# A three-layer graph network: the first layer's table as pairs of 16-bit parts, and eight node tiles of the next projection made during the first aggregation

## What is computed

```python
def reference(x, src, dst, edge_type_3, W0, b0, W1, q1, k1, b1, W2, q2, k2, b2):
    h = relu(layernorm(x))
    x = x + gcn(h)            # h @ W0, rows gathered by src, times dinv[src]*dinv[dst],
                              # summed by dst (with a loop per node), + b0
    h = relu(layernorm(x))
    h = elu(rgat_conv(h, W1, q1, k1, b1, heads=4))
    x = x + rgat_conv(h, W2, q2, k2, b2, heads=1)
    return x

def rgat_conv(x, W, q, k, b, heads):
    xr = einsum('nd,rdf->rnf', x, W)                   # 3 relations
    oi, oj = xr[etype, dst], xr[etype, src]
    alpha = leaky_relu(oi @ q + oj @ k, 0.2)
    e = exp(alpha - segment_max(alpha, dst)[dst])
    a = e / (segment_sum(e, dst)[dst] + 1e-16)
    return segment_sum(a * oj, dst) + b
```

## Time and profile before

| | us |
|---|---|
| median of 3 runs | 1609.46 |
| lowest, highest | 1606.19, 1611.54 |
| the profiled execution, its span | 1607.11, 1605.3 |
| first gather of the first aggregation | 199.7 |
| keys of layer 1 stored | 460.0 |
| first gather of the second aggregation | 780.1 |
| PE busy, share | 1453.7, 91% |
| GpSimd busy | 1000.9, 62% |
| DVE busy | 901.0, 56% |
| ACT busy | 274.0, 17% |

### The profile page before, as it was taken

How to read it: one execution, slowest core, us unless ns; L and a number is a source line. 1 busy time by engine, 2 the same in 40 slices (tenths; PEclk the granted TensorE clock), 3 DMA queues, 4 the chain that set the end, 5 groups by cost and what they waited for, 6 DMA issues and landing times.

```text
span 1605.3 us, 24837 instructions
## 1 busy us (share of the span) xinstructions
PE 1453.7 (91%) x6446; PEld 878.0 (55%) x6450; DVE 901.0 (56%) x2002; ACT 274.0 (17%) x709; POOL 1000.9 (62%) x1112
## 2 busy tenths in 40 slices
PE   4988999999978999999699999769996999899996
PEld 2545555555566555666455555455553655455553
DVE  8677722334455888888688878406324445223333
ACT  2545300000011333323000124410110011000000
POOL 1599277666537777882477777336656662777673
PEclk9988999999987999899799999858997999899998
DMA  8300498899831131111588888701231111889898
GB/s 319 118 20 21 125 315 305 291 316 312 270 102 23 51 110 47 40 37 41 169 303 278 285 262 257 241 3 32 59 111 31 40 43 50 286 298 308 281 303 269
DMA packets 86811, 271.80 MB, mean 169 GB/s; under 512 B 32156, under 2 KB 32531, under 8 KB 86743
## 3 DMA queue, kind: packets, MB, share of 16 engines
q0 software_dynamic: 51072, 199.44, 39.3%
q1 hardware_dynamic: 34807, 65.62, 11.4%
q10 hardware_dynamic: 864, 5.90, 1.0%
HBM read 239.28 MB, written 31.62 MB: 169 GB/s over the span
## 4 chain that ended last, share of the span: by engine, by line
PE 61%; DMA 14%; POOL 10%; issue 7%; DVE 5%; ACT 1%; DVEq 1%; SPq 0%; POOLq 0%; ACTq 0%; PEldq 0%
PE ps L1293 12%; PE ps L1320 12%; PE ps L1359 12%; DMA ring<-keys,idxr 8%; POOL ring L519 8%; PE ps L1361 6%; PE ps L1362 6%; PE ps L1190 5%; DMA ring<-rows,idxr 3%; PE ps L1111 1%; PE ps L1236 1%; PE ps L1153 1%; PE ps L1254 1%; DVE zw L1020 1%; DVE hn L1017 1%
## 5 line engine op out<-in xcount | busy, mean ns | idle before, releaser
L1320 PE MATMUL ps<-wreg,hT 128*128 128x384 f32 x1440 | 486.7, 501 | 7.3 <-PEq L1313 6.6
L519 POOL DMA_INDIRECT ring<-keys,idxr x312 | 319.2, 1023 | 189.1 <-DMA ring<-keys,idxr 73.6
L488 POOL DMA_INDIRECT ring<-rows,idxr x304 | 303.7, 999 | 168.8 <-PEq L1348 60.9
L1320 PEld LDWEIGHTS ps<-wreg,hT 128*128 128x128 f32 x1440 | 280.6, 196 | 202.2 <-issue 23.5
L1359 PE MATMUL ps<-ring,zw 128*128 x664 | 224.0, 495 | 15.6 <-DVE zw L1088 15.0
L1293 PE MATMUL ps<-ring,zw 128*128 x664 | 221.3, 495 | 9.6 <-DVE zw L909 9.6
L488 POOL DMA_INDIRECT ring<-rows,idx x152 | 144.7, 952 | 97.1 <-PE ps L1293 66.0
L1359 PEld LDWEIGHTS ps<-ring,zw 128*128 128x128 f32 x664 | 124.7, 191 | 108.7 <-issue 34.2
L1086 DVE TENSOR_TENSOR ring<-ring,al x166 | 159.2, 959 | 39.4 <-SPq L406 30.7
L1293 PEld LDWEIGHTS ps<-ring,zw 128*128 128x128 f32 x664 | 127.5, 193 | 98.1 <-issue 15.3
L1091 DVE TENSOR_SCALAR zw<-iota_f,tl,al 128x128 f32<-128x128 f32 x166 | 60.8, 368 | 154.7 <-PE ps L1362 129.7
(11 more groups left out here) (189 smaller groups left out, 1314.0 us busy)
## 6 DMA issues: line engine op xcount, KB each, us to landing
wreg<-in_L_gnn_W SPq DMA_DIRECT2D x11, 2304.0 KB, 9.8
rows<-stage SPq DMA_DIRECT2D x30, 386.0 KB, 2.8
rows<-stage SPq DMA_DIRECT2D x30, 384.5 KB, 2.9
stT<-targets_row ACTq DMA_DIRECT2D x6, 960.0 KB
ring<-keys,idxr POOLq DMA_INDIRECT x312, 2.5
ring<-rows,idxr POOLq DMA_INDIRECT x304, 4.5
rows<-stT SPq DMA_DIRECT2D x10, 384.0 KB, 2.9
xs<-in_x SPq DMA_DIRECT2D x3, 1152.0 KB, 13.4
```

The costliest lines, as they stand in the source:

```text
L488: nc.gpsimd.indirect_dma_start(ring[:, t % (2 * RING), 0:WIDTH[l]], None, rows[l], bass.IndirectOffsetOnAxis(idx[:, t:t + 1], 0)).then_inc ...
L519: nc.gpsimd.indirect_dma_start(kb[:, n % KSEMS, t % KB, 0:4], None, keys[l], bass.IndirectOffsetOnAxis(idxr[:, t:t + 1], 0)).then_inc(k_in ...
L1320: last = mm(ps[:, 2 * (nt % 2) + h, 0:HALF], hT[:, k, nt * P:(nt + 1) * P], wreg[:, r % 2, k, h * HALF:(h + 1) * HALF], start=(k == 0), st ...
```

## The change

1. **The first table in two 16-bit parts.** Per node and tile DVE takes the largest and smallest value of a row (`peaks`), makes a power of two from it (`units`), ACT writes the upper part as f16 (`upper_parts`), DVE the rest as a second f16 (`lower_parts`), and the row stored is upper and lower parts, 768 words as before, with the power of two in the 769th. The parts lie in `hT`, whose layout becomes node tile first. The first table is stored in three lots (`SPLITS`: node tiles 0 to 6, 7 and 8, 9). In the aggregation a slot tile is two one-hots in bf16 from a ring of four pairs, and four 16-bit products in place of two f32 ones; `dinv` of the source is in the parts already. DVE's one-hots no longer wait for `w_used`. A node's own row is added by PE (`open_own`), with a diagonal of the powers from DVE (`begin0`), in place of L886; the bias is added per node tile.
2. **Folds and weight products moved.** PE's folds of relation 0 stand behind the slot tiles of node tiles 0, 1 and 2 (`last_folds`); the wait for the parts stands ahead of node tile 0. `prepare(R - 1)` and the fill of `stage` move from the stage behind the aggregation to DVE's place behind node tile 0; `prepare(1)` now stands behind the lower parts, and the last weight load of layer 2 behind that.
3. **Early products.** In `early`, PE makes relation 0's products for node tiles 0 to 7 (`EARLY` = 8), each behind the turning of the next node tile; DVE makes `rstd` of a node tile with four Newton steps (`inverse_root`); ACT copies out and stores the row (`early_rows`). The stage behind starts with node tile 8. For layer 1 `MAX_AT` and `MASKS_AT` are set anew.

The core of the diff:

```diff
+          1: {17: (0,), 19: (1,), 21: (2,), 23: (3,), 24: (4,), 26: (5,), 27: (6,), 28: (7,), 29: (8, 9, 10, 11)}}
-MASKS_AT = [(SURE_PAIRS - 3) * (h + 1) // LAST_PAIRS_AT + 2 for h in range(LAST_PAIRS_AT)]
+EARLY = 8
+MASKS_AT = [(SURE_PAIRS - 3) * max(h + 1 - 2 * EARLY, 0) // (LAST_PAIRS_AT - 2 * EARLY) + 2 for h in range(LAST_PAIRS_AT)]
+SPLITS = ((0, 1, 2, 3, 4, 5, 6), (7, 8), (9,))
...
-        tbank = [2 * (n % 2) for n in range(NF)] + [0] * NT + [2 * (n % 2) for n in range(KT)] + [4] * NT + [4 + 2 * (n % 2) for n in range(NT)]
+        tbank = [2 * (n % 2) for n in range(NF)] + [0] * NT + [6] * KT + [4] * NT + [4 + 2 * (n % 2) for n in range(NT)]
...
+            def upper_parts(nt):
+                act.wait_ge(put_ready, [n for n, tiles in enumerate(SPLITS) if nt in tiles][0] + 1)
+                act.wait_ge(p_ready, 2 * nt + 2)
+                nc.scalar.activation(hT16[:, nt, :, 0, :], hw0[:, nt, :].rearrange("p (a c) -> p a c", a=2), ACT.Copy, scale=put[:, nt:nt + 1]).then_inc(hi_in, 1)
...
+            def early_rows(nt):
+                b = nt % 2
+                if nt == 0:
+                    act.wait_ge(wq2_done, R + 1)
+                if nt >= 2:
+                    act.wait_ge(stage_out[1][b], 16 * (nt // 2))
+                act.wait_ge(rstd1, nt + 1)
+                for h in range(2):
+                    act.wait_ge(p_ready, 2 * NT + 2 * nt + h + 1)
+                    nc.scalar.activation(stage_parts(b, h), ps[:, 6 + h, 0:HALF].rearrange("p (a c) -> p a c", a=2), ACT.Copy, scale=rstd[:, nt:nt + 1]).then_inc(early_in, 1)
+                act.wait_ge(early_in, 2 * nt + 2)
+                act.dma_start(rows[1][nt * P:(nt + 1) * P, :], stage[:, b, 0:WIDTH[1]]).then_inc(stage_out[1][b], 16)
...
+            def peaks(t):
+                dve.wait_ge(hw_ready, 2 * t + 2)
+                V.tensor_reduce(peak[:, 0, t:t + 1], hw0[:, t, :], AX.X, ALU.max)
+                return V.tensor_reduce(peak[:, 1, t:t + 1], hw0[:, t, :], AX.X, ALU.min)
...
+            def units(n, last):
+                at_ = slice(SPLITS[n][0], SPLITS[n][-1] + 1)
+                top, m, s = (pw[:, a, at_] for a in range(3))
+                link(last)
+                link(V.scalar_tensor_tensor(top, peak[:, 1, at_], -1.0, peak[:, 0, at_], ALU.mult, ALU.max))
+                link(V.tensor_scalar(m, top, TINY, SINK, ALU.max, ALU.mult))
+                link(V.scalar_tensor_tensor(s, m, LIFT, m, ALU.mult, ALU.add))
+                link(V.scalar_tensor_tensor(top, m, -LIFT, s, ALU.mult, ALU.add))
+                link(V.tensor_scalar(unit[:, at_], top, KEEP, None, ALU.mult))
+                link(V.reciprocal(m, unit[:, at_]))
+                if n == 0:
+                    dve.wait_ge(dinv_ready, 1)
+                V.tensor_tensor(put[:, at_], m, dinv[:, at_], ALU.mult).then_inc(put_ready, 1)
+                dve.wait_ge(put_ready, n + 1)
...
+            def lower_parts(t):
+                dve.wait_ge(hi_in, t + 1)
+                V.scalar_tensor_tensor(hT16[:, t, :, 1, :], hw0[:, t, :].rearrange("p (a c) -> p a c", a=2), put[:, t:t + 1], hT16[:, t, :, 0, :], ALU.mult, ALU.subtract).then_inc(split_in, 1)
...
+            for t in SPLITS[0][5:]:
+                last = peaks(t)
+            units(0, last)
+            for t in SPLITS[0][:-1]:
+                lower_parts(t)
+            for t in SPLITS[1]:
+                last = peaks(t)
+            units(1, last)
+            for t in SPLITS[0][-1:] + SPLITS[1]:
+                lower_parts(t)
+            units(2, peaks(NT - 1))
+            lower_parts(NT - 1)
             prepare(1)
             dve.wait_ge(s_bias[0], 16)
             dve.wait_ge(hn_ready, NT)
-            for j in range(NT):
-                last = V.tensor_tensor(xs[:, j, :], xs[:, j, :], bias[:, :], ALU.add)
-            link(last)
-
-
-            dve.wait_ge(dinv_ready, 1)
-            link(V.tensor_tensor(dinv2[:, :], dinv[:, :], dinv[:, :], ALU.mult))
-            for j in range(NT):
-                dve.wait_ge(hw_ready, 2 * j + 2)
-                last = V.scalar_tensor_tensor(xs[:, j, :], hw0[:, j, :], dinv2[:, j:j + 1], xs[:, j, :], ALU.mult, ALU.add)
...
+            def begin0(j):
+                V.tensor_scalar(own[:, j % 2, :], ident[:, :], unit[:, j:j + 1], None, ALU.mult).then_inc(own_in, 1)
+                link(V.tensor_tensor(xs[:, j, :], xs[:, j, :], bias[:, :], ALU.add))
...
+            def inverse_root(j):
+                v, y, a = vare[:, j:j + 1], rstd[:, j:j + 1], pw[:, 0, 0:1]
+                link(V.tensor_scalar(v, mv[:, j, 1:2], EPS_LN, None, ALU.add))
+                link(V.tensor_scalar(y.bitcast(I32), v.bitcast(I32), -0.5, float(0x5f375a00), ALU.mult, ALU.add))
+                for n in range(4):
+                    link(V.scalar_tensor_tensor(a, y, v, y, ALU.mult, ALU.mult))
+                    link(V.tensor_scalar(a, a, -0.5, 1.5, ALU.mult, ALU.add))
+                    last = V.tensor_tensor(y, y, a, ALU.mult)
+                    if n < 3:
+                        link(last)
+                last.then_inc(rstd1, 1)
...
                 with dve.Fori(bnd[j], bnd[j + 1]) as i:
+                    dve.wait_ge(g_in[0], 2 * i + (RING + 3))
                     for b in range(2):
-                        t = 2 * i + b
-                        if b == 0:
-                            dve.wait_ge(g_in[0], t + (RING + 3))
-                        dve.wait_ge(w_used[0], t + (2 * RING - 1))
-                        V.tensor_scalar(zw[:, 0, b, 0, :], iota_f[:, 0:P], targets_at(i, b), row_at(i, b, D, D + 1), ALU.is_equal, ALU.mult).then_inc(w_in[0], 1)
+                        V.tensor_scalar(onehot_at(i, b), iota_h[:, 0:P], targets_at(i, b), row_at(i, b, D, D + 1), ALU.is_equal, ALU.mult).then_inc(w_in[0], 1)
+                if j == 0:
+                    prepare(R - 1)
+                    V.memset(stage[:, :, :], 1.0).then_inc(wq2_done, 1)
                 if j >= 1:
...
-            for q in range(NF, NW):
-                n = q + NT
-                if q == NF + 1:
-                    pe.wait_ge(hw_ready, 2 * NT)
-                pe.wait_ge(t_free, NF + NT if q < NF + 2 else n - 1)
-                turn_block(q)
-                if q > NF:
...
+            def last_folds(first, end):
+                for q in range(first, end):
+                    if q == NF:
+                        pe.wait_ge(tlT_in, 2)
+                    pe.wait_ge(t_free, q + NT)
+                    turn_block(q)
+                    if q > first:
+                        wq_tile(q - 1)
+                wq_tile(end - 1)
+                if end == NW:
+                    fold(R - 1)
...
+            def open_own(j):
+                if j >= 2:
+                    pe.wait_ge(acc_free[0], j - 1)
+                pe.wait_ge(own_in, j + 1)
+                for a in range(2):
+                    for part in range(2):
+                        mm(ps[:, 2 * (j % 2) + a, 0:HALF], own[:, j % 2, :], hT16[:, j, a, part, :], start=(part == 0), stop=False, skip_group_check=True)
...
+            def early(nt):
+                pe.wait_ge(t_free, NW + NT + nt + 1)
+                for h in range(2):
+                    if nt >= 1:
+                        pe.wait_ge(early_in, 2 * (nt - 1) + h + 1)
+                    for k in range(KT):
+                        last = mm(ps[:, 6 + h, 0:HALF], hT[:, nt, k, :], wreg[:, 0, k, h * HALF:(h + 1) * HALF], start=(k == 0), stop=(k == KT - 1))
+                    last.then_inc(p_ready, 1)
...
+            pe.wait_ge(split_in, NT)
+            pe.wait_ge(hw_ready, 2 * NT)
             for j in range(NT + 1):
                 if j < NT:
-                    open_acc(0, j)
+                    open_own(j)
                     with pe.Fori(bnd[j], bnd[j + 1]) as i:
                         for b in range(2):
                             pe.wait_ge(w_in[0], 2 * i + (b + 1))
                             for a in range(2):
-                                last = mm(ps[:, 2 * (j % 2) + a, 0:HALF], zw[:, 0, b, 0, :], row_at(i, b, a * HALF, (a + 1) * HALF), start=False, stop=False, skip_group_check=True)
+                                for part in range(2):
+                                    last = mm(ps[:, 2 * (j % 2) + a, 0:HALF], onehot_at(i, b), parts_at(i, b, a, part), start=False, stop=False, skip_group_check=True)
                             last.then_inc(w_used[0], 1)
+                if j < 3:
+                    last_folds(NF + 2 * j, NF + 2 * j + 2)
                 if j >= 2:
                     for nt in ([j - 2] if j < NT else [j - 2, j - 1]):
                         to_features(1, nt)
+                        if 1 <= nt <= EARLY:
+                            early(nt - 1)
...
+                first = EARLY if l == 1 else 0
                 for r in range(R):
-                    for nt in range(NT):
+                    for nt in range(first if r == 0 else 0, NT):
                         n = r * NT + nt
```

(44 more changed lines are left out.)

71 lines of the change are left out of this document (47 added, 24 removed).

## The result

| | before | after |
|---|---|---|
| median, us | 1608.7 | 1667.7 |
| lowest, highest | 1606.2, 1611.5 | 1663.0, 1670.3 |
| profiled execution, its span | 1607.1, 1605.3 | 1667.7, 1664.6 |
| first gather | 199.7 | 205.2 |
| keys stored | 460.0 | 525.0 |

The account below looks back on a forecast made before the run. PE held most of the chain, but POOL was nearly as late in the aggregation, and POOL and DVE as late behind it. +8.4 + 10 + 30.5 - 3.2 = +45.7 on 1607.1 gave 1653 us, range 1614 to 1674.

Parts of the forecast that it names:

- Part 2: Before the first gather: preparing the 16-bit parts on ACT and DVE delays it by 8.4 us (4 to 14).
- Part 3: Node tiles 0 to 2: gathers at 1.25 us plus DVE pauses beyond the ring's cover, and weight load; +10 us (-5 to +18).
- The pause behind `prepare(R - 1)`: After node tile 0: DVE's 12.8 us of work, less 4.3 covered by the ring, leaves 8.5 us of standstill.
- a low clock: Node tiles 0 to 2: PE, busy only half the time, could drop to its lower clock level, 5 us more.
- Part 4: Node tiles 3 to 9: early f32 products add 62.9 us of PE work and the ring adds 18.4; +30.5 us (+6 to +42).
- Part 5: Stage behind the keys: POOL's gathers and DVE's passes stay, only waits for ACT's masks go; -3.2 us (0 to -15).
- (1): Stage behind: PE alone bounds it, so 62.9 us leave it instead of 3.2; 1593 us, chance 0.08.
- (2): Aggregation: the ring covers the pauses, low ends of the terms, +2 us in all; 1609 us, chance 0.12.
- (3): Node tiles 0 to 2: 16-bit one-hots lengthen 90 gathers by 0.27 us each, +24 us; 1677 us, chance 0.08.
- The port rule: Gathers: DVE's two-port mode blocks GpSimd's descriptor writes; by one row 0.08 us per gather, 7 us in all.
- (4): Slot tiles: 16-bit products not four times shorter, as weight loads aren't hidden; +12 us, 1665 us, chance 0.06.

Follow-up runs that it names:

- kernel 2: Changed kernel without early products, and DVE's last weight products back behind the keys; 1612.9 us, ratio 1.003 to the kernel before.
- kernel 8: Changed kernel with the last weight load beside the first gathers cut to 128 of 768 rows (work left out); 1662.7 us, ratio 1.031.
- kernel 1: Changed kernel without early products, maxima back where they stood before; 1622.5 us, ratio 1.007 to the kernel before.
- Kernel 4: Changed kernel with the second half of early products made behind the next node tile's sixth slot tile, last two whole; 1653.2 us, ratio 1.027.
- Kernels 5 to 7: Changed kernel with four early products (1654.5 us); those plus the old maxima table's placing (1685.2); eight early products, maxima two projections sooner (1691.7).
- kernel 9: No early products, weight products back behind the keys, and the last weight load issued by ACT in node tile 3; 1609.8 us, ratio 1.001.

## Why the prediction held, and where it was short

- **Part 2 (before the first gather), +8.4 predicted.** +5.5 in this execution; 208.2 in the mean of eleven kernels against 199.7 and 201.4 is +7.6. Right, near enough: DVE's last lower part ended at 201.3, where the sum had 203.8.
- **Part 3 (node tiles 0 to 2), +10 predicted, +16.8 measured.** The pause behind `prepare(R - 1)` was right (8.5; kernel 2 gives 9.2 back). By the prediction's own terms node tile 0, from the first gather, had 83.5 us and took 88.9; node tile 1 had 30.4 and took 34.2; node tile 2 had 27.2 and took 25.0. Of node tile 0's excess the weight load is 2.3 (2 taken of 0 to 7.8; 4.3 in kernel 8). The rest isn't isolated: the prediction put up to 5 us on a low clock here, granted 0.86, and nothing on the gathers beside `prepare(1)`, which took up to 1.57 us.
- **Part 4 (node tiles 3 to 9), +30.5 predicted, +42.7 measured.** The mechanism was right: PE's 62.9 us land in a stretch where PE and POOL are evenly matched, and kernel 1 shows 48.3 of them there. The term that was mis-sized is PE's own work: 134.7 at least by the sum, 144.9 in the trace. By groups, which overlap, its slot tiles take 59.6 and not 50.2, its own rows 6.4 and not 4.6, its other work 3.4 more. I put this on the clock, granted 0.91: a burst ends in a wait for the ring and the next begins at the 1.2 GHz level. Kernel 4 fits that, with the same products in 136.7 us at 0.99. The Trainium skill, "TensorE: Matmul & The Clock Gate", section "HAM oscillation — how this bites in real kernels", describes this: bursts of products between waits for DMA, each beginning throttled. The trace agrees, by the 0.50 in the row above; I had weighed the lower clock for part 3 alone. The idle time was right (24.2 predicted, 26.7 measured).
- **Part 5 (the stage behind), -3.2 predicted, -0.7 measured.** Right in the point that mattered: POOL's scores and DVE's passes set its end, not PE; kernel 1, with all 30 projections in the stage, has 320.0 too. The 4.5 us of waits for ACT's masks did go, but DVE waited a little longer for POOL (16.8 for 15.5), whose last score came no sooner behind the keys. Kernels 5 to 7 add what the prediction had not seen: the stage is level only while the table of maxima suits the number of projections. The changed kernel's table did.
- **Rivals.** (1), a stage bound by PE, needed 60 us less there; it fell by 0.7. (2), covered pauses, needed node tiles 3 to 9 under 140. (3), longer gathers: the pitch stayed 1.25. The port rule of the Trainium skill, "SBUF — State Buffer", section "SBUF: two separate sides", cited ahead, has no case in the 16-bit one-hots here: the gathers beside them keep their 0.95. (4), products not four times shorter: 0.1675 us each at full clock refutes it as put, but at the lower level they take 0.34, and PE's excess in part 4 is about what this rival priced (+12). That the time fell inside the range owes something to this: its place was forecast, the size of PE's work was not.

## What to carry to other kernels

Before work is moved out of a stage, ask what is late next there; before it is moved into another, ask whether that stage's engines are evenly matched: then each microsecond arrives nearly whole (48.3 of 62.9 here), and a faster product beside it earns only the little by which its engine was behind. If such work must go in, put it in the middle of a stream that waits for transfers, in pieces that the ring can cover, and not at the end of a group, where the ring is full (here 17 us of 48 for the same work). A table that places one engine's turns in another's order is fitted to a count; move the count and the table together.

## Unexpected in the hardware's behaviour

- A shorter product can go with a lower clock: with PE busy for 90 of 148 us instead of 126 of 131 the granted clock was 0.86 instead of 0.97, and eight 16-bit products took 2.74 us behind a wait, 1.3 in a stream.
- A weight load of 2.4 MB beside the gathers costs some 4 us of them at their start (4.3 in kernel 8); moved behind node tile 3, it made node tile 4 longer by 3 us (kernel 9).
- DVE's weight products (f32, two operands) beside gathers lengthen these from 0.95 to 1.45 us; the 16-bit one-hots don't.
